# One attention stage of a four-layer block: probabilities are divided before they are turned, and the values come out turned

## The reference, cut to what matters

```python
x = x + jnp.tanh(g_xattn[2]) * _L2_xattn_ref(_layernorm(x), ctx_1024, mask, Wq, Wkv, Wout, b_out)

def _L2_xattn_ref(q, context, mask, Wq, Wkv, Wout, b_out):   # 16 heads of 64
    k, v = jnp.split(context @ Wkv, 2, -1)
    attn = jnp.einsum('bhid,bhjd->bhij', heads(q @ Wq), heads(k)) * 64 ** -0.5
    attn = jnp.where(mask[:, None, None, :], -jnp.inf, attn)
    attn = jax.nn.softmax(attn, axis=-1)
    out = jnp.einsum('bhij,bhjd->bhid', attn, heads(v))
    return merge(out) @ Wout + b_out
```

## Time and profile before

| | us |
|---|---|
| median of three runs (lowest, highest) | 1562.96 (1562.08, 1563.18) |
| the profiled execution: its time | 1561.37 |
| its span, first to last instruction | 1559.6 |

### The profile page before, as it was taken

One profiled execution on the slowest core, in us unless ns is written; L12 is line 12 of the kernel. 1 busy time (PEld: TensorE's weight loads), 2 busy tenths in 40 slices (PEclk: granted clock), 3 DMA queues, 4 the chain that ended last, 5 costly groups with the idle time before them and its releaser, 6 DMA issues. The chain is left out here.

```text
span 1559.6 us, 26943 instructions
## 1 busy us (share of the span) xinstructions
PE 1352.5 (87%) x8843; PEld 1045.2 (67%) x8843; DVE 845.7 (54%) x2280; ACT 710.9 (46%) x1593; POOL 146.7 (9%) x256
## 2 busy tenths in 40 slices
PE   6766799999996899689999997984699987999995
PEld 5642477777775487578888886973477764766664
DVE  4549777777763554645555553346687762122224
ACT  4331676776762302245555552442355542333343
POOL 1010000000001000000000002005244421000000
PEclk9869899999996999889999997995699987999998
DMA  8000000000000000000000004002000000000000
GB/s 335 1 1 0 1 1 1 1 1 2 1 1 1 1 1 0 1 1 1 2 1 2 1 1 115 8 1 108 1 1 1 0 1 1 1 1 1 1 1 28
DMA packets 6427, 24.52 MB, mean 16 GB/s; under 512 B 797, under 2 KB 1311, under 8 KB 5418
## 3 DMA queue, kind: packets, MB, share of 16 engines
q1 hardware_dynamic: 6314, 23.03, 4.3%
HBM read 21.98 MB, written 1.05 MB: 15 GB/s over the span
## 5 line engine op out<-in xcount | busy, mean ns | idle before, releaser
L1317 DVE SCALAR_TENSOR_TENSOR XN<-bank,gate,XN 128x128 f32<-128x128 f32 x256 | 89.8, 351 | 224.8 <-PE bank L1281 222.2
L1297 ACT ACTIVATE e_hidden<-bank,small 128x512 f32<-128x512 f32 x152 | 104.4, 687 | 214.6 <-PE bank L1269 214.5
L767 PE MATMUL bank<-a_va,a_pT 128*128 128x65 f32 x1024 | 129.4, 269 | 0.8 <-ACT a_pT L933 0.5
L1281 PEld LDWEIGHTS bank<-attention_weights,e_hidden 128*128 128x128 f32 x1024 | 119.2, 192 | 14.8 <-issue 14.8
L767 PEld LDWEIGHTS bank<-a_va,a_pT 128*128 128x128 f32 x1024 | 124.4, 192 | 2.3 <-ACT a_pT L933 0.8
L1019 DVE TENSOR_REDUCE a_mx<-bank 128x4 f32<-128x512 f32 x128 | 87.8, 686 | 64.9 <-PE bank L807 64.4
L1269 PE MATMUL bank<-XNT,attention_weights 128*128 128x512 f32 x256 | 121.2, 606 | 1.2 <-PEq L541 1.2
L1281 PE MATMUL bank<-attention_weights,e_hidden 128*128 128x128 f32 x1024 | 119.3, 275 | 0.0
L933 ACT ACTIVATE a_pT<-bank 128x512 f32<-128x512 f32 x128 | 76.6, 599 | 41.8 <-PE bank L840 41.8
L1027 DVE TENSOR_TENSOR a_shifted<-bank,a_mx 128x512 f32<-128x512 f32 x128 | 88.3, 690 | 3.4
L1912 PEld LDWEIGHTS bank<-blk_va,blk_pT 128*128 128x128 f32 x512 | 64.5, 194 | 33.5 <-issue 21.9
(11 more groups left out here) (353 smaller groups left out, 2646.3 us busy)
## 6 DMA issues: line engine op xcount, KB each, us to landing
attention_weights<-in_a SPq DMA_DIRECT2D x2, 2048.0 KB, 11.7
mod_ring<-in_mod_weights SPq DMA_DIRECT2D x4, 576.0 KB
ctx_both<-in_ctx SPq DMA_DIRECT2D x1, 2048.0 KB, 9.2
attention_weights<-in_up SPq DMA_DIRECT2D x1, 2048.0 KB, 8.2
attention_weights<-in_down SPq DMA_DIRECT2D x1, 2048.0 KB, 12.7
down<-in_down SPq DMA_DIRECT2D x1, 1536.0 KB, 18.2
down<-in_mod_weights SPq DMA_DIRECT2D x2, 576.0 KB
X<-in_x SPq DMA_DIRECT2D x4, 256.0 KB, 3.9
```

Source lines behind the costliest of these rows:

```text
L767: last = pe.matmul(value_bank[:, j * (W + 1):(j + 1) * (W + 1)], pT[:, i.slot(2), j * 128:(j + 1) * 128], va[:, p, g // 2 * 8 + 2 * j + g ...
L1281: last = pe.matmul(down_bank[j][:, 0:width], layer[0:rows, f, j * 128:(j + 1) * 128], down(g, f), start=f == 0, stop=f == NB - 1)
L1297: act.activation(hidden[0:rows, p, f, :], up_bank_of(i, f)[0:rows, :], function, bias=up_bias(g, f)).then_inc(hidden_ready, 1)
L1317: dve.scalar_tensor_tensor(out=total, in0=down_bank[j][:, e * D:(e + 1) * D], scalar=gate_column(k, 4 * q + j, g * per_group + e), in1=tot ...
```

## The change

`stage_attention_2` calls a new function, `stage_turned_attention`, in place of `stage_head_attention`. The first attention stage and all else stay. In the new function:

- DVE sums the exponentials (`total_up`: a reduction over 128x512 and a reciprocal of 128x4); `invert_sums` and `normalise_o` are gone, and so is the column of ones in `va` with its memset.
- POOL multiplies the 128x512 exponentials by the reciprocals into a new double buffer `pn` (`normalise_p`), and `turn_p` turns `pn`. The turned probabilities have four buffers in place of two.
- `values` runs for two items at once, in every second step: eight matmuls with 64 value columns stationary, placed on columns 0 to 63 of the array for the even head and on columns 64 to 127 for the odd one (`tile_position=(0, 64 * a)`), and `pT` moves with 128 columns. The result is already turned, so `turn_o` with its two transposes an item is gone, and `keep_o` copies 128x512 for two items straight from the values' bank in place of 128x256 an item.
- The lags are longer: turned probabilities 7 in place of 6, values 9 in place of 8, output 11 in place of 10, norm 12 in place of 11. With them `values` falls in the steps with scores (A, C), `keep_o` in B and D, the output in C, and `norm.rstd` in D.
- POOL's copies are made at set steps between the divisions in place of running ahead.

```diff
-        lag = {"keep_qk": 1, "scores": 4, "project_v": 4, "subtract": 4, "exponentials": 5,
-               "turn_p": 6, "keep_p": 7, "values": 8, "turn_o": 10, "out": 10, "normalise": 11, "turn_x": 11}
+        lag = {"keep_qk": 1, "scores": 4, "project_v": 4, "subtract": 4, "exponentials": 5, "sums": 5,
+               "turn_p": 7, "keep_p": 8, "values": 9, "keep_o": 10, "out": 11, "normalise": 12, "turn_x": 12}
...
+            def normalise_p(i):
+                m, p = i.number, i.slot(2)
+                await_count(pool, inverted, m + 1)
+                if i.older_than(2):
+                    await_count(pool, p_turned, m - 1)
+                pool.tensor_tensor(pn[:, p, :].rearrange("p (h s) -> p h s", h=4),
+                                   probs[:, p, :].rearrange("p (h s) -> p h s", h=4),
+                                   rec[:, p, :].unsqueeze(2).to_broadcast([128, 4, S]), ALU.mult).then_inc(p_normed, 1)
...
+            def values(i):
+                m, (b, g), p = i.number, i.part(4), (i.offset // 4) % 2
+                await_count(pe, p_kept, m + 1)
+                await_count(pe, v_kept, m // 2 + 1)
+                if i.older_than(2):
+                    await_count(pe, o_kept, m // 2)
+                for j in range(4):
+                    for a in range(2):
+                        last = pe.matmul(value_bank[64 * a:64 * a + 64, j * 128:(j + 1) * 128],
+                                         va[:, p, g // 2 * 8 + 2 * j + a, :],
+                                         pT[:, (i.offset - 1 + a) % 4, j * 128:(j + 1) * 128],
+                                         start=True, stop=True, tile_position=(0, 64 * a))
...
+            def keep_o(i):
+                m, (b, g), p = i.number, i.part(4), (i.offset // 4) % 2
+                await_count(act, weighted, m + 1)
+                if g == 1 and i.older_than(8):
+                    await_count(act, y_done, b - 1)
+                act.activation(oT[:, p, g // 2 * 512:g // 2 * 512 + 512], value_bank[:, :], ACT.Copy).then_inc(o_kept, 1)
...
+            def total_up(i):
+                m, p = i.number, i.slot(2)
+                await_count(dve, exped, m + 1)
+                dve.tensor_reduce(total[:, p, :], probs[:, p, :].rearrange("p (h s) -> p h s", h=4), AX.X,
+                                  ALU.add).then_inc(totalled, 1)
+                await_count(dve, totalled, m + 1)
+                if i.older_than(2):
+                    await_count(dve, p_normed, m - 1)
+                dve.reciprocal(rec[:, p, :], total[:, p, :]).then_inc(inverted, 1)
...
-        stage_head_attention(nc, k, "a2", k.a2[:, 0:1024], k.a2[:, 1024:2048], k.a2[:, 2048:3072],
+        stage_turned_attention(nc, k, "a2", k.a2[:, 0:1024], k.a2[:, 1024:2048], k.a2[:, 2048:3072],
                              k.a2[:, 3072:4096], k.bias[0:1, 128:256], 2, key_mask=mask_row)
```

285 lines of the change are left out of this document (added).

## The result

| | us |
|---|---|
| before, median of four runs (lowest, highest) | 1562.52 (1561.61, 1563.18) |
| changed, median of four runs (lowest, highest) | 1543.39 (1540.88, 1543.88) |
| ratio, with its 95% interval | 0.9875 (0.9858 to 0.9892) |
| profiled execution of the changed kernel: time, span | 1543.88, 1542.1 |

The changed kernel is 1.2% faster. The forecast was 1548.6 with 1541 to 1556 as its own range, so the time lies inside the range and the forecast was 5 us too high.

What follows compares the result with a forecast made beforehand. PE, busy 29.70 of 30 us, bounds the kernel; afterwards waits on keep_qk also count. Gains of 2.1 (fill), 8.2 (twelve batches), 3.0 (step 64 to 66) and 1.1 (tail) make 14.4 us: 1548.6, range 1541 to 1556.

Steps and rivals of the forecast that it cites:

- V: One values piece for two items, sixteen loads on two column tiles running side by side: 1.10 us, possibly 1.0 to 1.90.
- half A to C: From scores of step A to those of C, through project_v, keep_v, exponentials, keep_qk and project_qk: 5.67 + V = 6.77 us.
- half C to A: From scores of step C to those of A, through output, DVE's L113, ACT's L126, keep_qk and project_qk: 7.85 + V = 8.95.
- batch: Scores of one step A to the next: 15.72 us instead of 16.40, 1.75 of them PE waiting; twelve batches gain 8.2.
- step 64 to 66: Stretch without project_qk near the stage's end: held by DVE's maxima, five operations and a reciprocal, 4.9 us, gain 3.0.
- second rival: Values' column tiles don't run side by side: V = 1.90, 24.8 us more, 1573.4, slower than before; chance 0.12.
- drain of 0.2: Full array drain behind each values piece at a change of tiling form: would add some 0.2 to V, 6 us in all.
- Third rival, PE full: PE's waits on keep_qk vanish: 12 batches gain 2.43 us each, fill 5.3, end 4.1, time 1524; chance 0.08.
- PE's sum of 13.97: PE's own pieces in one batch without waits: 13.97 us, 2.43 less than 16.40; stage would gain nearly 40 us.
- Fill: From scores of step 8 to those of step 16: 28.16 us instead of 30.24, gain 2.1.
- Tail: From step 66 to the last output: some 18.0 us instead of 19.06, gain 1.1, least certain, from -2 to +3.
- The cover: POOL's division, 1.04 us, lies at least 4.9 us ahead of the turn that needs it: hidden by 3.8 us.

Runs made afterwards that it cites:

- The order experiment: Changed kernel with the eight value matmuls reordered, four on the left column tile, then four on the right: 1562.14 us, ratio 0.9994 to the kernel before.

## Why the prediction was right

| step | before | predicted | measured |
|---|---|---|---|
| V, one piece of values | | 1.10 | 1.02 |
| half A to C, half C to A | | 6.77, 8.95 | 6.70, 8.85 to 8.89 |
| batch | 16.40 | 15.72 | 15.55 |
| step 8 to 16 | 30.24 | 28.16 | 27.91 |
| step 64 to 66 | 7.89 | 4.9 | 5.19 |
| step 66 to the last output | 19.06 | 18.0 | 19.23 |
| gain up to the last output | | 14.4 | 15.05 |
| behind the last output | 619.15 | unchanged | 616.7 |

- **V.** The scores piece was the right neighbour. V came out 0.08 lower, near the lower bound of 1.0. The order experiment shows why the second rival failed, and that it was a real one: without neighbours on different tiles V is 1.51 and nothing is gained. No drain of 0.2 came on top of V: the 0.17 us of idle time behind the values' loads (ahead of 754.39) are part of the 1.02. The Trainium skill ("TensorE: Matmul & The Clock Gate", Part 3: Packing small matmuls) ties the overlap of loads to different row groups. Here the row groups are the same and the order of the tiles still makes 1.02 out of 1.51, so something overlaps, and in this form the measurement decides against that rule.
- **The halves.** Both walks hold link by link. From A to C: 1.21 + 1.02, `keep_v` 1.17 behind `project_v` (763.29 to 764.46), `keep_qk` 1.49 behind that (765.95), L860 0.71 later, scores 1.09 later: 6.69 of 6.70. From C to A: L113 at s + 5.18, L126 0.98 later, `keep_qk` 0.96 after that, then 0.69 and 1.08. The one link read differently is how `project_v` and the output share 2.95 us: the output's first load comes 0.54 behind `project_v`, not 0.86, and L113 2.41 behind that, not 2.10. (One load goes ahead; the other fifteen follow at 755.36, 0.97 behind `project_v`.) The sum is the same. The batch is 0.17 shorter than predicted, nearly all of it 2 x 0.08 of V; over twelve batches that is 2.0 us.
- **Third rival, PE full.** It fails in the change as made and is right as a bound: PE's sum of 13.97 was measured as 14.14 once the waits were gone.
- **Fill.** 27.91 against 28.16: the three halves' share of V again.
- **Step 64 to 66.** The size is nearly right, the reason is not. I had DVE hold it. In the trace PE's `turn_p` waits there for ACT's `keep_p` (0.83 us at 905.61), which stands behind `keep_v`, and that behind `project_v`: 1.21 + 1.02 + 1.16 + 0.50 + 0.70 + 0.59 is 5.18. It is the loop of the first half once more, without `project_qk` in it, and should have been seen. The kernel with V at 1.51 bears it out: there the same stretch takes 5.67, longer by the 0.49 of V. So the term came near by luck.
- **Tail.** The gain of 1.1 did not come (19.23 against the predicted 18.0, and 19.06 before). The update of x is where it was put (5.18 against 5.3), and the last division nearly so (10.30 against 10.6). Then values that start at 917.11 cost 1.90 instead of 1.02, at a granted clock of 0.50, behind pieces between which PE had waited (0.97 ahead of 914.36). That is 0.88 of the missing 1.2. Charging no clock was right for the middle of the stage (1.00 throughout) and wrong for its end. The rest is small errors of the walk in both directions.
- **POOL and DVE.** The division took 1.04 and PE's matmuls of `turn_p` never waited for it. The cover was named rightly, but the other way in which POOL can cost time, holding DVE, stood nowhere in the prediction. It cost nothing here only because L135 starts as the division ends.
- **The sum.** 14.4 predicted and 15.05 measured up to the last output, with 2.45 behind it to make the span's 17.5. Against the forecast that is 0.65 and 2.45, or 3.1 us of the span. The other 2.1 of the 5.2 by which the median came out lower is how profiled executions stand to medians: I added 1.6 us for it, and the changed kernel's profiled execution lies 0.5 above its median. Neither the 2.45 nor the 2.1 was foreseen, so they are chance as far as the forecast goes.

## What to carry to other kernels

When an engine at 99% loses work, walk the loop of waits through the other engines' lists before counting the saving: here a saving of 2.43 us a batch on PE was worth 0.85. A one-line change of an engine's order released 0.68 more; a lag one step longer with one more buffer, tried on its own, released 1.41. Before an item is moved a step later, list every buffer whose release it carries, and who stands behind the writer of that buffer. A wait in a full list can cost more than its length: in the kernel with values in B and D and two buffers a clock of 1.2 GHz behind some of the waits cost 0.91 us a batch. And keep small matmuls on two tiles alternating in program order, since four in a row on one tile gave the whole gain back.

## What had not been expected of the hardware

- Work on two column tiles that share all rows overlaps when the instructions alternate: sixteen loads in 0.85 us. Four matmuls in a row on one 64-column tile still cost less than full-width ones, 94 ns a record against 111.
- A VectorE `tensor_scalar` of 128x128 between SBUF tiles takes 1156 ns instead of 346 beside a GpSimd `tensor_tensor` of 1.04 us, while reductions and a subtraction that reads PSUM keep their 675 to 688 ns.
- Waits of 1.36 and 0.38 us in an otherwise full list were followed by a stretch at 1.2 GHz in seven batches of one stage, and not in the batches between them.
- A stage's thin end can leave TensorE at 1.2 or at 2.4 GHz, and the same work behind the stage's last output took from 613.2 to 619.15 us.
